# Self-attention: the rotation's sum on GpSimd instead of VectorE, and the five engines' orders written anew

## The reference

```python
attn_in = _adaln(x, cond, ln1_w, ln1_b, g1_w, g1_b, b1_w, b1_b)
x = _attn(attn_in, attn_in, sa_wq, sa_wkv, sa_wo, sa_bo) + x
cross_in = _adaln(x, cond, ln1_w, ln1_b, g1_w, g1_b, b1_w, b1_b)
ctx_n = _ln(context, ca_lnc_w, ca_lnc_b)
x = _attn(cross_in, ctx_n, ca_wq, ca_wkv, ca_wo, ca_bo) + x
ffn_in = _adaln(x, cond, ln2_w, ln2_b, g2_w, g2_b, b2_w, b2_b)
h = jax.nn.gelu(ffn_in @ ff_w1 + ff_b1, approximate=False)
x = h @ ff_w2 + ff_b2 + x

def _rope(x, sin, cos):
    s = sin[None, None]
    c = cos[None, None]
    xe = x[..., ::2]
    xo = x[..., 1::2]
    re = xe * c - xo * s
    ro = xe * s + xo * c
    return jnp.stack((re, ro), axis=-1).reshape(x.shape)

def _attn(xq, ctx, wq, wkv, wo, bo):
    q = _heads(xq @ wq)
    k, v = jnp.split(ctx @ wkv, 2, axis=-1)
    ...
    q = _rope(q, sq, cq)
    k = _rope(k, sk, ck)
    sim = jnp.einsum('bhnd,bhmd->bhnm', q, k) * DH ** (-0.5)
    a = jax.nn.softmax(sim, axis=-1)
    o = jnp.einsum('bhnm,bhmd->bhnd', a, v)
    o = o.transpose(0, 2, 1, 3).reshape(xq.shape[0], xq.shape[1], MID)
    return o @ wo + bo
```

## Time and profile before

| | |
|---|---|
| Time, median of 3 runs (lowest to highest) | 2023.34 us (2021.45 to 2027.23) |
| The profiled execution | 2026.98 us, span 2025.2 us |
| Granted TensorE clock, mean | 0.981 |
| Busy in the span: PE, PEld, DVE, ACT, POOL | 96%, 66%, 78%, 48%, 63% |
| Self-attention stage | about 36 to 444 us |

### The profile page before, as it was taken

How to read it: one execution, slowest core, us unless ns; L and a number is a source line. 1 busy time by engine, 2 the same in 40 slices (tenths; PEclk the granted TensorE clock), 3 DMA queues, 4 the chain that set the end, 5 groups by cost and what they waited for, 6 DMA issues and landing times.

```text
span 2025.2 us, 53734 instructions
## 1 busy us (share of the span) xinstructions
PE 1934.8 (96%) x20832; PEld 1335.1 (66%) x20832; DVE 1569.7 (78%) x2292; ACT 980.8 (48%) x1580; POOL 1266.5 (63%) x819
## 2 busy tenths in 40 slices
PE   5888999987999999999999999999999999999987
PEld 2666777743667666766667666677666776667753
DVE  3888888857887888888888878888888888888832
ACT  2544555533454445544454544554545454445533
POOL 5666656421766676766767667676676766766650
PEclk8999999996999999999999999999999999999989
DMA  4322223211111111111111111111111111111100
GB/s 150 108 79 74 74 79 111 77 35 41 51 56 56 48 54 51 57 55 48 52 54 55 57 48 50 56 55 57 49 52 54 55 57 49 52 54 55 51 14 21
DMA packets 110439, 118.90 MB, mean 59 GB/s; under 512 B 26480, under 2 KB 74736, under 8 KB 110064
## 3 DMA queue, kind: packets, MB, share of 16 engines
q1 hardware_dynamic: 110192, 115.46, 17.3%
HBM read 36.71 MB, written 1.05 MB: 19 GB/s over the span
## 4 chain that ended last, share of the span: by engine, by line
PE 74%; POOL 8%; issue 6%; DVE 4%; DMA 4%; ACT 1%; SPq 1%; POOLq 0%; DVEq 0%; ACTq 0%
PE S L1200 19%; PE OB L1212 17%; PE PB L1147 9%; PE PB L1158 9%; PE S L1173 7%; POOL psum_acc L612 3%; DMA swapped<-turned 2%; POOL psum_acc L578 2%; PE PB L1221 2%; PE PB L1137 2%; POOL KL L571 2%; PE PB L1231 1%; DMA qswapped<-qturned 1%; PE PB L1182 1%; PE PB L1112 1%
## 5 line engine op out<-in xcount | busy, mean ns | idle before, releaser
L612 POOL TENSOR_TENSOR psum_acc<-psum_acc,P 124x1024 f32<-124x1024 f32 (+1 forms) x320 | 689.7, 2155 | 93.6 <-ACT P L743 75.5
L743 ACT ACTIVATE P<-S 124x1024 f32<-124x1024 f32 (+1 forms) x448 | 431.4, 963 | 465.8 <-PE S L1200 465.0
L927 DVE TENSOR_REDUCE mxc<-S 128x2 f32<-128x1024 f32 x384 | 468.6, 1220 | 89.9 <-PE S L1173 89.4
L1212 PE MATMUL OB<-P,V 124*64 124x256 f32 (+1 forms) x3328 | 428.9, 381 | 0.0
L605 POOL TENSOR_TENSOR psum_acc<-P 124x1024 f32<-124x1024 f32 x64 | 152.6, 2384 | 332.6 <-ACT P L743 332.6
L1212 PEld LDWEIGHTS OB<-P,V 124*64 124x64 f32 (+1 forms) x3328 | 223.9, 136 | 130.6 <-issue 38.1
L1200 PE MATMUL S<-QH,KH 64*124 64x256 f32 (+1 forms) x1664 | 254.6, 301 | 3.0 <-ACT P L743 3.0
L632 ACT ACTIVATE V<-PB 124x512 f32<-124x512 f32 (+1 forms) x320 | 156.6, 489 | 179.3 <-PE PB L1158 88.2
L893 DVE TENSOR_TENSOR turned<-PB,rope 128x512 f32<-128x512 f32 (+1 forms) x256 | 145.9, 570 | 116.8 <-PE PB L1147 116.7
L1200 PE MATMUL S<-QL,KH 64*124 64x256 f32 (+1 forms) x1664 | 234.8, 277 | 0.0
L1200 PE MATMUL S<-QH,KL 64*124 64x256 f32 (+1 forms) x1664 | 234.7, 277 | 0.0
(11 more groups left out here) (122 smaller groups left out, 3088.7 us busy)
## 6 DMA issues: line engine op xcount, KB each, us to landing
swapped<-turned SPq DMA_DIRECT2D x512, 128.0 KB, 2.1
kv_w<-sa_kv_dram SPq DMA_DIRECT2D x64, 128.0 KB, 2.3
qswapped<-qturned SPq DMA_DIRECT2D x128, 64.0 KB, 1.9
kv_w<-ca_kv_dram SPq DMA_DIRECT2D x64, 96.0 KB, 2.2
ctxT_all<-ctx_dram SPq DMA_DIRECT2D x8, 624.0 KB, 5.3
q_w<-sa_wq_dram SPq DMA_DIRECT2D x64, 64.0 KB, 2.0
q_w<-ca_wq_dram SPq DMA_DIRECT2D x64, 64.0 KB, 1.9
o_w<-ca_wo_dram SPq DMA_DIRECT2D x64, 64.0 KB, 2.0
```

What stands on the lines that cost most here:

```text
L612: pool.tensor_tensor(acc, acc, P_of(J, c)[0:rows, :, 0:w], ALU.add).then_inc(x.acc, 1)
L743: act.activation(P_of(J, c)[0:rows, :, 0:w], SP[0:rows, :, 0:w], ACT.Exp, scale=SCALE).then_inc(x.e, 1)
L927: dve.tensor_reduce(mxc[:, t, :, c:c + 1], MP[:, :, 0:w], AX.X, ALU.max).then_inc(x.am, 1)
L1212: ins = pe.matmul(OB[half(h), 0:N], Vb[J % 2][0:w, t, half(h)], P_of(J, c)[0:w, h, k * N:(k + 1) * N], start=(t == 0), stop=(t == len(a_.t ...
```

## The change

`rotate` goes from VectorE to GpSimd, with the same operands and now in place in `QK`. `cosines` writes `QK` in SBUF instead of the bank, no longer waits for `turn`, and takes over the wait for l of J - 2. `project_v` waits for c instead of r. The five orders are written anew; the largest lead stays 3 steps (SP's weights), the lag grows from 1 to 2.

```diff
--- before.py
+++ after.py
@@ -81,10 +81,10 @@
     CTX = B * M + 56
     TOK = CTX - B * CW
     SELF = Stage("sa",
-                 "qk+3 v+2 sum+-1 p+-1 s a+2 ct m+1 o+-1",
-                 "r+2 am+1 t+3 rc+-1 dv+-1 c+3 ad+-1 cn",
-                 "e mr+1 ca cn ve+3 h+3 oe",
-                 "l+2 cp f cq",
+                 "qk+2 v+1 o+-2 m a+1 p+-1 sum+-1 s ct",
+                 "ad+-2 t+2 c+2 am+1 rc+-1 dv+-1 cn",
+                 "ve+1 mr oe+-1 e ca cn h+2",
+                 "l+1 r+2 cp f cq",
                  "w+3 x+2")
     CROSS = Cross("ca", DC, M, 124, 512,
                   "a3 k0+1 v3+-1 p1+-1 a4 s3+-1 q+1 p2+-1 a5 s4+-1 v0 k1+1 s5+-1 a6 v1 k2+1 p3+-1 m "
@@ -571,13 +571,19 @@
                     pool.tensor_tensor(low(J, 0, 0, W), QK[J % 2][:, :], high(J, 0, 0, W).bitcast(F32), ALU.subtract
                                        ).then_inc(z.l, 1)
 
+                def rotate(J, _):
+                    i = J % SLOTS
+                    wait(pool, z.c, J + 1)
+                    wait(pool, z.swap[i], J // SLOTS * 32 + 32)
+                    pool.tensor_tensor(QK[J % 2][:, :], QK[J % 2][:, :], swapped[i][:, :], ALU.add).then_inc(z.r, 1)
+
                 def fold(J, _):
                     P = PR[J % 4]
                     wait(pool, z.e, J + 1)
                     wait(pool, z.sum, J - 1)
                     pool.tensor_tensor(added_up(J), P[:, :, 0:N], P[:, :, N:2 * N], ALU.add).then_inc(z.f, 1)
 
-                run_steps(SELF, in_order(SELF.pool, {"l": low_parts, "f": fold, "cp": context_first,
+                run_steps(SELF, in_order(SELF.pool, {"r": rotate, "l": low_parts, "f": fold, "cp": context_first,
                                                      "cq": context_second}))
 
             def cross():
@@ -825,16 +831,9 @@
                                       ).then_inc(z.t, 1)
 
                 def cosines(J, _):
-                    wait(dve, z.t, J + 1)
-                    bank = halves(KB[J % 2][:, :])
-                    dve.tensor_tensor(bank, bank, both(ropeq[:, 0:N]), ALU.mult).then_inc(z.c, 1)
-
-                def rotate(J, _):
-                    i = J % SLOTS
-                    wait(dve, z.c, J + 1)
-                    wait(dve, z.swap[i], J // SLOTS * 32 + 32)
                     wait(dve, z.l, J - 1)
-                    dve.tensor_tensor(QK[J % 2][:, :], KB[J % 2][:, :], swapped[i][:, :], ALU.add).then_inc(z.r, 1)
+                    dve.tensor_tensor(halves(QK[J % 2][:, :]), halves(KB[J % 2][:, :]), both(ropeq[:, 0:N]), ALU.mult
+                                      ).then_inc(z.c, 1)
 
                 def maximum(J, _):
                     wait(dve, z.a, J + 1)
@@ -866,7 +865,7 @@
                         wait(dve, cx.std, g // 2 + 1)
                         dve.reciprocal(cstd[:, columns], cstd[:, columns]).then_inc(cx.inv, 1)
 
-                run_steps(SELF, in_order(SELF.dve, {"cn": context_inverse, "t": turn, "c": cosines, "r": rotate, "am": maximum,
+                run_steps(SELF, in_order(SELF.dve, {"cn": context_inverse, "t": turn, "c": cosines, "am": maximum,
                                                     "rc": invert, "dv": divide, "ad": add}))
                 dve.wait_ge(z.added, B)
 
@@ -1031,7 +1030,7 @@
 
                 def project_v(J, _):
                     loaded(J)
-                    wait(pe, z.r, J + 1)
+                    wait(pe, z.c, J + 1)
                     for t in range(2):
                         at = batch(J) * N + t * D
                         for h in range(2):
```

## The result

The changed kernel takes 2032.9 us (median of 8 runs, 2030.1 to 2036.6), the kernel before 2023.5: ratio 1.0048, 95% interval 1.0039 to 1.0057. Forecast were 2015.5 us, with 2004 to 2030 as the range. The changed kernel is 0.5% slower; the time lies outside the range, and it moved the other way than forecast.

The account below looks back on a forecast made before the run. VectorE was taken to bound self-attention steps without transposes, TensorE those with them. Stretches -0.3, 0 and -3.8, squares +2, drain -1.5, start -4 gave -7.6, say -8 us: 2015.5 us, range 2004 to 2030.

Parts of the forecast that it names:

- steps with transposes unchanged at 5.61 and 4.88: Self-attention steps with a large or small transpose: TensorE is the bound and keeps 5.61 and 4.88 us.
- 4.68 us of own work without them: Steps without transposes: TensorE's own work is 5.20 less 0.52 us of waiting, 4.68 us.
- The loop of the rotation: Projection, turn, swap, GpSimd's sum, through scores to the projection two steps on: some 9.2 us over two steps, 4.6 a step.
- GpSimd can't be packed: Rival, chance 0.16: late swaps or pieces leave holes in GpSimd's row; at 0.5 us on each of 39 steps, 2035 us.
- ScalarE's work for the context: Squares ahead of the high parts on ScalarE: 6 of 8 cost 0.3 us each, +2 us (0 to 6).
- GpSimd becomes the bound: Steps with context pieces: GpSimd's work sets 5.46 us a step for J = 4 to 23, 5.57 for J = 23 to 38.
- The mistake in the output products: Steps with an output product: where GpSimd binds, TensorE's slack absorbs some, so 3.1 us extra, with a transpose 4.1.
- the sum's time on GpSimd: One 128x512 sum a step on GpSimd, taken like its fold: 1.27 us.
- cosines into SBUF: VectorE's cosines writing SBUF as turn does: 678 to 691 ns, no dearer than now.
- VectorE's falling off the path: VectorE's step becomes 4.45 us without the sum and its wait; it waits in most steps.
- 4.2 us from output product to m: Output product on TensorE, then m waiting for its addition: 3.48 + 0.73 us.
- the drain's and start's direction: Both ends of the self-attention get shorter: drain -1.5 us, start -4 us (bounds +0.6 and -6).

Follow-up runs that it names:

- experiments 1 and 2: Kernel before, TensorE's context transposes moved between scores and first scores: 2029.0 us, ratio 1.0029; the same with m also ahead of the first scores: 2032.8 us, 1.0056.
- experiment 5: Changed kernel with all its new orders, but the rotation's sum done by VectorE again: 2041.9 us, ratio 1.0096 to the kernel before.
- experiment 8: Changed kernel with GpSimd's context pieces cut to one column of tiles each: 2029.8 us, ratio 1.0018 to the kernel before.
- experiment 4: Changed kernel with the first scores directly ahead of the scores in TensorE's order: 2058.3 us, ratio 1.0173 to the kernel before.

## Why the prediction was wrong

**The step that failed** is TensorE's: "steps with transposes unchanged at 5.61 and 4.88", and 4.68 us of own work without them. The sum counted the products of a step and took their slots over from the old order. Measured are 5.96, 5.20 and 4.95 us. 24 large and 8 small transposes at 0.35 and 0.32 us are 11 us over the slots of before. Against the forecast they are some 9 of the 19.6 us by which the stretches miss, an estimate: 5.1 from J = 38 to 63, where it had 10 steps at 5.61 and 5 at 4.88, and 3.9 from J = 23 to 38, where the sum had not TensorE's 5.61 but GpSimd's 5.57 for 10 steps of 5.96. From J = 4 to 23 there are no transposes, and what follows made the miss of 4.4 us. That the order of the groups sets their slots is shown in the kernel before (experiments 1 and 2), and that steps with transposes are TensorE's in the new orders, whoever makes the sum, by experiment 5. The new order was in the prediction's own rows; which waits moved was read from it, and not which groups were parted.

**Second, the swap.** The loop of the rotation was put at 9.2 us over two steps, with 2.74 us from turn's end to the landing; 2.73 was right as the usual time. The prediction took it as fixed. It was not in the kernel before either: there VectorE's sum came 2.77 us after turn's end, 0.04 us behind the usual landing, and 17 of its sums between 70 and 430 us waited. The view puts them down to the cosines; but in the 16 of them that the timeline shows singly the sum starts 0.4 to 0.6 us after the swap's last packet, so it was the swap, on the engine that set the pace there:

```profile
DVE QK L837 <- DVE PB L830: 8.7, 17, 0.8
```

Two things differ. In the kernel before, after the start, no fetch of 16 KB began between 1.6 and 2.0 us after turn's end, so the longest wait was 0.8 us; in the changed kernel six did, and why they fall there is open. And the first scores stood 1.3 us behind the high parts before (384.18 against 382.85 in one step), while now it is 0.4 (387.83 against 387.44): less room for a late sum. The rival "GpSimd can't be packed" named the sum's wait for a late swap, and its mark, GpSimd waiting for the swap, was seen. But most of its waits cost nothing, late swaps are 4.9 us, and eight of them came with VectorE's sum as well (experiment 5). That its 2035 us is near the 2032.9 measured is in good part luck, since it had TensorE's steps unchanged. Its other half, the pieces, cost a few us and not the most (experiment 8).

**ScalarE's work for the context** was put too low. The squares cost 0.9 us for each of four seen in experiment 8, and 0.9 to 1.7 in the changed kernel, with its pieces, not the 0.3 taken, since the high parts stand behind them and the first scores behind those. The roots with their table load (J = 14 and 41) were not in the sum at all; against the kernel before each is 0.9 us longer.

**"GpSimd becomes the bound"** in steps with pieces, 5.46 and 5.57 us, was wrong for the changed kernel: at 89% and 83% busy it waits for swaps, and many steps with pieces take TensorE's 4.95. The mistake in the output products comes with it (8.6 us where GpSimd binds; 9.8 and 10.0 measured): nothing of them was absorbed. In the old orders with the sum behind the fold GpSimd's share does cost, +5 us in each of the first two stretches.

**Right were** the sum's time on GpSimd (1276 ns in the mean, taken as 1.27), cosines into SBUF (681 ns), VectorE's falling off the path, 4.2 us from output product to m, the drain's and start's direction, both too small, and that VectorE's products and GpSimd don't hold each other up.

Not settled: how the 17.6 us lost divide between TensorE's 11, late swaps, ScalarE's work and pieces, which share steps, and which the light steps, 4.95 for 5.20, partly pay back. No run has the groups unparted with everything else of the changed kernel as it is; the one that tried (experiment 4) made every step 5.93 us.

## What to carry to other kernels

When an order is rewritten, count the places where a group of products of one row shape stands between groups of another, and read each group's slot with its neighbours; it isn't a constant. Where a transfer is used by an in-order engine as soon as it usually lands, its usual time isn't enough: here 6 swaps in 60 landed over 1.7 us late, and five of them made a long step. Look also at what stands ahead of the critical row on an engine with time to spare, here ScalarE. Undo orders and move apart: here each alone cost 9 us or more, and the gain lay only in the start and the end.

## What the runs showed of the hardware

- The first scores, products of 64 rows, took 0.32 us beside the scores, which are such products too, and 0.44 between products of 128 rows. With the transposes ahead and m behind the step grew by 0.18 us; with m ahead and the projection behind, where those two were longer by 0.1 and 0.05 us, by 0.33 (experiments 1 and 2).
- A fetch of 16 KB of instructions that began 1.7 to 2.0 us after turn's end, among the packets of a swap, came with a landing at 4.5 to 5.0 us instead of 2.7, in all six cases of the changed kernel. That the fetch is the cause is read from the times of the packets; no run moved the fetches.
- In experiment 5 VectorE's sum reads two operands in SBUF: 797 ns in the mean against 689 with one in PSUM, and GpSimd's fold beside it 1638 ns against 1274. The Trainium skill's SBUF — State Buffer (Who interferes with whom) says that an instruction of VectorE with two SBUF inputs contends with one of GpSimd that reads SBUF; the trace agrees.
